# One TensorE step for the next group's transposes and this group's products, with one semaphore, in edge phases 2 and 3

## What is computed

```python
# layer 2
se = jnp.concatenate([h[src], eh], axis=-1)                 # 64 + 64 features
msg = leaky_relu(se @ W_msg)
q = jnp.concatenate([qrh, qeh], axis=-1) @ W_q / temp
k = se @ W_k
att = jnp.sum(q * k, axis=-1)                               # softmax over the edges of a node
agg = segment_sum(alpha[..., None] * msg, dst)
# layer 3
combined = jnp.concatenate([node_features[src], edge_features], axis=-1)   # 64 + 32
for l in range(2):
    h = relu(combined @ msg_w1[l] + msg_b1[l]); msg = msg + (h @ msg_w2[l] + msg_b2[l])
agg = segment_sum(msg, dst)                                 # divided by the degree
```

## Time and profile before

| what | value |
|---|---|
| time, median of 3 runs | 12250.41 us |
| span of the profiled execution | 12212.0 us |
| edge 2, about 5266 to 8700 | 3434 us, PE busy 1423.24 us |
| edge 3, about 8960 to 11960 | 3000 us, PE busy 967.92 us |
| cycle of a chunk in edge 2 (6520.13 to 6581.58) | 61.45 us |
| cycle of a chunk in edge 3 (9850.20 to 9903.83) | 53.63 us |
| one gather: first issue to the end of the last (6520.13 to 6554.80) | 34.67 us |

### The profile page before, as it was taken

How to read it: one execution, slowest core, us unless ns; L and a number is a source line. 1 busy time by engine, 2 the same in 40 slices (tenths; PEclk the granted TensorE clock), 3 DMA queues, 4 the chain that set the end, 5 groups by cost and what they waited for, 6 DMA issues and landing times. The chain is left out here.

```text
span 12212.0 us, 65741 instructions
## 1 busy us (share of the span) xinstructions
PE 2780.2 (23%) x15715; PEld 2525.3 (21%) x15715; DVE 4710.0 (39%) x6608; ACT 3336.3 (27%) x4637; POOL 6789.5 (56%) x6997
## 2 busy tenths in 40 slices
PE   2000000011000000044444444444333332333333
PEld 1000000010000000034334333333232222322233
DVE  3455555555666666432222222222231111111113
ACT  0222222233222222132222222222242232232231
POOL 6666666657777777644444444444435544544543
PEclk6555555555555555577666667667655555555556
DMA  6232323312222222222222222222111211211121
GB/s 270 91 99 95 98 95 99 99 47 74 98 98 94 98 93 96 69 75 76 76 76 76 76 76 76 75 73 79 39 42 55 63 62 55 63 62 59 59 62 52
DMA packets 366486, 982.75 MB, mean 80 GB/s; under 512 B 163828, under 2 KB 173582, under 8 KB 351652
## 3 DMA queue, kind: packets, MB, share of 16 engines
q1 hardware_dynamic: 135572, 667.06, 14.4%
q0 software_dynamic: 224608, 290.88, 9.4%
q10 hardware_dynamic: 6192, 23.73, 0.5%
HBM read 582.50 MB, written 398.69 MB: 80 GB/s over the span
## 5 line engine op out<-in xcount | busy, mean ns | idle before, releaser
L771 POOL DMA_INDIRECT se<-x_table,edge_ix x1512 | 1428.3, 945 | 1867.2 <-PEq L1343 1397.1
L771 POOL DMA_INDIRECT comb<-x_table,edge_ix x1512 | 1428.8, 945 | 1468.3 <-DMA edge_ix<-in_src 1010.4
L771 POOL DMA_INDIRECT g<-x_table,edge_ix x1512 | 1585.4, 1049 | 512.2 <-issue 512.2
L771 POOL DMA_INDIRECT qv<-qv_table,edge_ix x1484 | 1406.5, 948 | 681.1 <-issue 445.6
L889 DVE TENSOR_TENSOR_SCAN edge_val<-edge_bank,edge_val 128x464 f32<-128x464 f32 (+1 forms) x715 | 687.4, 1031 | 2469.3 <-ACT edge_val L1597 2462.9
L1565 PE MATMUL h_ps<-w_hidden,edge_comb_t 97*128 97x128 f32 x3136 | 699.3, 394 | 1924.3 <-issue 964.5
L899 ACT ACTIVATE edge_sums<-edge_val 128x1904 f32<-128x1904 f32 (+3 forms) x219 | 1107.0, 5055 | 0.0
L1454 DVE TENSOR_TENSOR edge_product<-mk_ps,edge_q_now 128x256 f32<-128x256 f32 x392 | 166.4, 424 | 2364.2 <-ACT edge_msg L1393 2344.8
L1565 PEld LDWEIGHTS h_ps<-w_hidden,edge_comb_t 97*128 97x128 f32 x3136 | 613.2, 291 | 2000.2 <-ACT edge_comb_t L1592 1009.0
L1353 PE MATMUL mk_ps<-w_mk,edge_se_t 128*128 128x128 f32 x3136 | 545.9, 329 | 1659.7 <-issue 1412.0
L1353 PEld LDWEIGHTS mk_ps<-w_mk,edge_se_t 128*128 128x128 f32 x3136 | 483.1, 235 | 1709.1 <-issue 1424.3
(11 more groups left out here) (416 smaller groups left out, 9145.2 us busy)
## 6 DMA issues: line engine op xcount, KB each, us to landing
sums<-edge_sums SPq DMA_DIRECT2D x56, 1848.0 KB
sums<-edge_sums SPq DMA_DIRECT2D x55, 1792.0 KB, 6.6
sums<-edge_sums SPq DMA_DIRECT2D x56, 1008.0 KB
sums<-edge_sums SPq DMA_DIRECT2D x55, 924.0 KB, 3.7
edge_k<-k_edges SPq DMA_DIRECT2D x56, 896.0 KB
edge_bond<-in_edge_attr SPq DMA_DIRECT2D x56, 896.0 KB
edge_eh<-in_edge_attr SPq DMA_DIRECT2D x56, 896.0 KB
edge_qr<-in_edge_attr_n SPq DMA_DIRECT2D x56, 896.0 KB
```

Source lines behind the costliest of these rows:

```text
L771: e.indirect_dma_start(self.gather_into(u, j), None, self.gather_from, bass.IndirectOffsetOnAxis(ap=now[:, j:j + 1], axis=0))\
```

## The change

`turned` and `multiplied` are replaced by one semaphore, `stepped`. TensorE posts once for t(0), once for each pair of t(c+1) and m(c), and at the end once for m(5) with t(6) and once for m(6): 8 posts a chunk. The order of TensorE's instructions and all buffers stay. move(c) waits for post c+1 of its chunk, which is that of t(c) and m(c-1); take(c) waits for post c+2, which holds m(c). Edge 3 is changed in the same way.

```diff
-    per = 2 * quads
+    per, steps = 2 * quads, quads + 1
...
-        turned = ph.sem("turned")
+        stepped = ph.sem("stepped")
...
-        multiplied = ph.sem("multiplied")
...
-            e.sem_inc(multiplied, 2)
...
-                last.then_inc(turned, 1)
                 if c == quads - 1:
                     e.drain().then_inc(ph.rows_free[b], 1)
                     e.drain().then_inc(ph.attr_free[b], 1)
+                return last
...
-                last.then_inc(multiplied, 1)
+                return last
...
-                    turn(i, b, 0)
+                    turn(i, b, 0).then_inc(stepped, 1)
                     for c in range(quads):
                         if c + 1 < quads - 1:
                             turn(i, b, c + 1)
-                        multiply(i, b, c)
+                        last = multiply(i, b, c)
                         if c + 1 == quads - 1:
-                            turn(i, b, c + 1)
+                            last = turn(i, b, c + 1)
+                        last.then_inc(stepped, 1)
...
             def move(i, b, c):
-                e.wait_ge(turned, at(i, per, n + 1))
-                e.wait_ge(multiplied, at(i, per, n + 1))
+                e.wait_ge(stepped, at(i, 2 * steps, b * steps + c + 1))
...
             def take(i, b, c):
-                e.wait_ge(multiplied, at(i, per, n + 3))
+                e.wait_ge(stepped, at(i, 2 * steps, b * steps + c + 2))
```

## The result

The changed kernel takes 12,485.59 us, median of 4 runs (12,482.51 to 12,490.51), beside 12,253.15 us for the kernel before: a ratio of 1.0192 (95% interval 1.0177 to 1.0206), slower by 232 us. The forecast was 12,458 us, 208 slower.

The account below looks back on a forecast made before the run. Waits bound the kernel: POOL's gather restart behind a TensorE and ScalarE chain. Edge 2's +178 and edge 3's +30 make 208; 12,212 + 208 + 38 = 12,458 us, own range 12,380 to 12,600, 8-in-10 range 12,080 to 12,640.

Parts of the forecast that it names:

- What bounds the kernel: Edges 2 and 3: no engine is full, waits decide; POOL's gather restart ends a 61.45 us cycle in edge 2.
- the release: Edges 2 and 3: point 4.6 us after the gather's last instruction, when TensorE's late signals have all reached their readers.
- Fewer posts: Edges 2 and 3: 14 posts a chunk become 8, 672 increments fewer; costed at 0, an estimated 18 us at most.
- Move waits for the product: Edge 2: move's two copies start only when the product has ended; +3.14 us a chunk, +178 us in all.
- the two distances behind it: Edge 2, behind lay_out: m(5), t(6) and the restart keep their distance, so 0.
- rival 2: Edges 2 and 3: slower still, through TensorE's low clock (12,740 us) or m(3) running too late (12,600); chance 0.10.
- Edge 3: +0.49 a chunk: Edge 3: move(4) now lies ahead of take(3) and lay_out; +0.49 us a chunk, +30 us with the last chunk.
- The sum: Edge 2's +178 us and edge 3's +30 us: 208 us slower, 12,458 us.
- the one ahead of m(2): Edge 2: gap from m(1)'s end to m(2)'s start goes from 1.50 to 1.75 us, +0.25 a chunk.
- the low end: Edge 2: some chunks get m(0) a little before the release, half of the +0.9 gaps are hidden; about +130 us total.
- Rival 1: Gathers of edges 2 and 3: each post has its own price, so fewer are faster; 11,750 to 12,080 us, chance 0.22.
- Rival 3: Edges 2 and 3: no change, copies hidden because something else sets the restart; 12,250 to 12,290 us, chance 0.06.

## Why the prediction was right

*What bounds the kernel.* Right: the gather's restart, set by the chain from the release. Taking work out of this chain (lay_out in edge 2) gave 206 of 208 expected, and putting work into it cost what it takes.

*Fewer posts: 0.* Right in its result: the runs with the old posts and with 7,840 more show it directly. The reason that I gave for it is not shown. It rested on two intervals in node 3 (2.80 us a matmul, both times) and on m(0) of edge 2. In edge 3 of the same trace, over 53 cycles, the eight products m(2) were read 9.9 us after t(3) on average, and the four transposes t(4) 8.1 us after m(2): no one price a matmul fits both of these and node 3. What the lateness counts stays open.

*Move waits for the product: +3.14 us a chunk in edge 2.* Right in place. In the cycle shown it was 0.16 short: m(1) +0.97; m(2) +0.27 in its start (1.77 less 1.50), and 0.08 back, as it ran wholly at the high clock; m(3) +0.97; lay_out +0.95; the two distances behind it, which I had put at 0, +0.02 and +0.18. Together that is 3.30 us (25.45 less 22.15), the hundredths being rounded. The missing term is the 0.18 from m(5) to the restart, 5.28 against 5.10 us, counted from the row of 6016.34 above and from this one of the kernel before:

```profile
6576.48 2.05 PE L1353 MATMUL mk_ps<-w_mk,edge_se_t 128*128 128x128 f32 x8 [3.29 <-ACT edge_q_t L1384]
```

All of it is in m(5) itself, which took 3.43 us before and 3.61 after: its clock rose to the higher level one product later. This is rival 2's cost at a small size.

*Edge 3: +0.49 a chunk.* The waits say 0.40 and the cycles 0.47; the phase alone gave +30.8 us (20 to 43), where +30 was forecast.

*The sum.* 55 x 3.30 = 182, with 5 for the last chunk and 31 for edge 3, is 218 of the 232 us. The rest is that one cycle is not the mean. Over its 53 full cycles edge 2 takes 61.45 us where only edge 3 was changed and 65.04 where only edge 2 was, on the same chip: +3.59, and 55 x 3.59 + 5 = 202 us, where the phase alone gave 201.6. The term that I had too small is the one ahead of m(2). I took +0.25 from a cycle in which t(3) fills that gap at the low clock (1.50 us). In 17 of the 53 unchanged cycles of that run the gap was 0.8 to 0.9 us, as t(3) already ran at the higher level, and the mean was 1.26; after the change it is 1.77 in every cycle, so the mean loss is 0.51. In 11 of these 17 m(5) too ran wholly at the higher level, in 2.02 us (granted clock 1.00 from 6593.90 to 6595.90), and they lasted 59.3 to 60.0 us:

```profile
6593.88 1.13 PE L1353 MATMUL mk_ps<-w_mk,edge_se_t 128*128 128x128 f32 x8 [3.25 <-ACT edge_q_t L1384]
```

In the changed kernel no m(5) took under 2.75 us, and no cycle was under 64.7 us. So the later move costs the copies, and besides it loses the cycles in which TensorE's clock was up early. Why the clock rises earlier in some cycles stays open.

The other thing that I expected at the low end, m(0) being read ahead of the release in some chunks, explains none of this. In the trace of before it was so in four of the five cycles under 60 us; in the run with edge 3 alone changed it was so in none. One effect of the change I had left out: take(5) shares its post with t(6) and waits for it, so that the next chunk starts 0.7 us later (7.3 us after the gather's start in place of 6.6). It is off the path: with only the waits moved a chunk starts at 6.6 us as before, and no cycle was under 64.7 us either.

*The rivals.* Rival 1 didn't come: lay_out in edge 3 is 40.6 us after the gather's start. Its evidence, the 8.41 us of t(4)'s four transposes, is real, and no run here explains it. Rival 2 came only at a small size, in m(5) and ahead of m(2): the clock stayed at 1.00 in the gaps, and in the cycle of edge 3 shown m(3) ran before the release. In that cycle m(2) was read 33 us after the gather's start (9909.55), where the forecast had 22; the median over 53 cycles is 25, and in one of them (57.25 us) m(3) did miss the release. Rival 3 fell with the first row of waits.

## What to carry to other kernels

Before two signals are merged into one, ask what the reader of the earlier one does in the meantime: if it is work that ran beside the later one, this work now stands on the path, once for each step, and the price is its duration, less the idle time that stood there already (here 0.97 us at three steps and 0.27 at one, in the cycle shown). Fewer semaphore increments were worth nothing here, where no engine waits for the increments themselves. Where signals of one engine are held while another issues a long stream, put work that needs no such signal into the stream, and break the stream once or twice; here both together were worth 10%, where the change to the signals lost 2%.

## What the runs showed of the hardware that was not expected

While GpSimd issues indirect gathers, TensorE's signals reach their readers late: m(0) of edge 2, whose successors had ended by 6534.75, was read at 6559.43, over 24 us later. Not all of them are: t(0) of the same chunk, 10.6 us into the gather, was read as soon as it had ended,

```profile
6530.69 0.60 ACT L1383 ACTIVATE edge_se_t<-se_ps 128x512 f32<-128x512 f32 x1 [2.27 <-PE q_ps L1339]
```

and ScalarE's signals are not late (rows 9 and 10: its copy ends at 12041.39, TensorE's product behind it starts at 12041.44, in the same gather). The lateness does not go with the increments (7,840 more of them moved the mean read of m(2) by 1 us, within its spread, and the release not at all); with what it goes is open. A wait of 2.0 us in the middle of 28 gathers was enough for m(0)'s signal to come 14 us earlier, though gathers were issued again 3.4 us before it came. The ends of matmuls are modelled in the trace, so it can't tell a late signal from a late result. Two such waits in each gather made the whole kernel 10% faster together with the moved lay_out.
